# One joined first stage, its loads in order of need, and identity matmuls at the end of two attentions

## What is computed

```
x = x + L0_attn(layernorm(x))                 # softmax attention through 64 landmarks
x = x + L0_xattn(layernorm(x), ctx_512)       # 16 heads of 16: causal self-attention + attention to the context
x = x + L0_ffn(layernorm(x))                  # linear layer, x and weight rounded to a 6-bit grid in blocks of 32
x = x + L1_attn(layernorm(x))                 # attention on hyperbolic distances, masked by a threshold
x = x + L1_xattn(layernorm(x), ctx_512)       # 16 heads of 32, self and cross, each with an MLP
x = x + L1_ffn(layernorm(x))                  # 8 experts, the best 2 of each row
```

```
y = softmax(mask(q k^T / 4)) v                # first attention, 512 keys
y = y + softmax(qc kc^T / 4) vc               # second attention, 1024 keys of the context
return y @ Wp + bp
```

## Time and profile before

| | |
|---|---|
| median of 3 runs | 4172.58 us (4172.36 to 4176.27) |
| the profiled execution | 4168.0 us, span 4166.0 us |
| PE busy | 3411.4 us, 82% |
| DVE busy | 2071.5 us, 50% |
| ACT busy | 1641.3 us, 39% |
| POOL busy | 914.9 us, 22% |
| mean granted clock of PE | 0.914 |

### The profile page before, as it was taken

How to read it: one execution, slowest core, us unless ns; L and a number is a source line. 1 busy time by engine, 2 the same in 40 slices (tenths; PEclk the granted TensorE clock), 3 DMA queues, 4 the chain that set the end, 5 groups by cost and what they waited for, 6 DMA issues and landing times. The chain is left out here.

```text
span 4166.0 us, 56508 instructions
## 1 busy us (share of the span) xinstructions
PE 3411.4 (82%) x21678; PEld 1873.9 (45%) x21678; DVE 2071.5 (50%) x4222; ACT 1641.3 (39%) x2355; POOL 914.9 (22%) x955
## 2 busy tenths in 40 slices
PE   2888788898897688898887788988877888956997
PEld 2423554326325455245334535264235543345886
DVE  3464656553564654634556654634646556530111
ACT  1344654242343833333344742433437542411221
POOL 0210642001201822011104622012006420131111
PEclk9989899999998799999898899999997999967999
DMA  4121102201202012111112012011211121034444
GB/s 83 39 57 61 16 23 64 64 20 32 74 12 76 1 44 72 34 36 44 46 31 57 1 44 86 20 42 39 57 61 16 31 69 50 26 117 156 167 166 166
DMA packets 242482, 239.79 MB, mean 58 GB/s; under 512 B 111726, under 2 KB 209244, under 8 KB 239900
## 3 DMA queue, kind: packets, MB, share of 16 engines
q1 hardware_dynamic: 231344, 214.02, 17.7%
q10 hardware_dynamic: 7116, 11.77, 0.9%
q0 software_dynamic: 3744, 10.26, 0.6%
HBM read 167.24 MB, written 68.76 MB: 57 GB/s over the span
## 5 line engine op out<-in xcount | busy, mean ns | idle before, releaser
L864 ACT ACTIVATE prob<-psum 128x1024 f32<-128x1024 f32 x384 | 372.2, 1021 | 507.8 <-PE psum L782 507.8
L1202 ACT ACTIVATE prob<-psum 128x1024 f32<-128x1024 f32 (+3 forms) x384 | 331.5, 914 | 420.5 <-PE psum L1122 420.5
L910 DVE TENSOR_REDUCE scr<-psum 128x1 f32<-128x512 f32 x576 | 368.9, 685 | 194.2 <-PE psum L769 190.5
L1241 DVE TENSOR_REDUCE stats<-psum 128x1 f32<-128x512 f32 (+3 forms) x576 | 333.4, 619 | 158.4 <-PE psum L1110 153.8
L1122 PE MATMUL psum<-stack 32*128 32x512 f32 (+3 forms) x1536 | 210.7, 619 | 49.1 <-ACT prob L1202 41.2
L779 PE MATMUL psum<-stack 32*128 32x512 f32 x1536 | 226.6, 660 | 15.3 <-ACT prob L864 10.4
L400 PE MATMUL psum<-ident 128*128 128x128 f32 x1832 | 224.2, 280 | 14.6 <-PEq L1830 9.6
L400 PEld LDWEIGHTS psum<-ident 128*128 128x128 f32 x1832 | 216.5, 195 | 25.3 <-issue 24.4
L812 PE MATMUL psum<-prob,ones_f 128*32 128x512 f32 x1536 | 201.4, 592 | 0.0
L1137 PE MATMUL psum<-prob,vbig 128*32 128x512 f32 (+3 forms) x1536 | 191.9, 573 | 4.3 <-ACT prob L1202 4.3
L2741 PE MATMUL psum<-xgT,ew 128*128 128x256 f32 x736 | 167.8, 387 | 18.0 <-DVE xgT L2789 18.0
(11 more groups left out here) (469 smaller groups left out, 6488.2 us busy)
## 6 DMA issues: line engine op xcount, KB each, us to landing
ew<-in_L_ffn_W SPq DMA_DIRECT2D x46, 1024.0 KB, 7.5
stack<-q_terms SPq DMA_DIRECT2D x144, 128.0 KB, 2.6
w_mlp<-in_L_xattn_a_li_w SPq DMA_DIRECT2D x16, 1024.0 KB, 7.0
q_terms<-parts SPq DMA_DIRECT2D x96, 128.0 KB, 2.2
stack<-k_terms SPq DMA_DIRECT2D x72, 128.0 KB, 3.0
w_mlp<-k_terms SPq DMA_DIRECT2D x36, 256.0 KB, 4.5
w_mlp<-a_terms SPq DMA_DIRECT2D x36, 256.0 KB, 5.0
a_keys<-stack SPq DMA_DIRECT2D x4, 2048.0 KB, 6.3
```

The lines of the kernel that those rows point to most:

```text
L864: act.activation(prob[:, i % 4, :, :], psum[:, 2 * p:2 * p + 2, :], ACT.Exp, scale=scale).then_inc(exped, 1)
L910: dve.tensor_reduce(found[:, c:c + 1], ring(i), AX.X, ALU.max).then_inc(freed, 1)
L1202: act.activation(prob[:, i % 4, :, q0:T], psum[:, 2 * p:2 * p + 2, q0:T], ACT.Exp, scale=scale).then_inc(exped, 1)
L1241: dve.tensor_reduce(found[:, c:c + 1], ring(i)[:, 0:keys_of(t)], AX.X, ALU.max).then_inc(freed, 1)
```

## The change

**First piece.** The stages "clear", "load" and "qw" become one, "start" (from L266 of the new file on). Its engines do the following.

- SP issues 37 DMAs in this order: the matrix of the linear layer, `x`, the three weights of the first attention, the four weights of the attentions with heads of 16 as whole rows into a scratch tile (`unpadded`), and then 28 "late" ones. These count on the semaphore `loads`, and nobody waits for it in this stage.
- ACT issues the context, three biases and 21 small vectors (rows, no longer columns), and then copies the four weights from the scratch tile into their padded places, and the columns from PSUM.
- POOL clears the padded tiles and makes the masks; DVE fills, copies, and rounds the matrix as soon as that has landed; PE transposes the small vectors and the matrix.

The late loads are waited for by SP in "Asm", ahead of `load_kv`.

**Second piece.** At the end of `narrow_heads`, thus in "Ba" and "Bca", PE gets 3, 2 and 6 calls of `keep_running`.

```
+            sp.dma_start(xa[:, 0:KT, :], dram["L0_ffn_weight"]...).then_inc(linear_in, 16)
+            load_x(sp, slice(0, 1))
+            load_qkv(sp, 0)
+            for w, source, raw in heads:
+                sp.dma_start(raw[:, 0:w.shape[1], :], source).then_inc(raw_in, 16)
+            late(wBv[:, :, :], dram["L0_xattn_Wv"].rearrange("(k p) n -> p k n", p=P))
+            late(wBcv[:, :, :], dram["L0_xattn_Wcv"].rearrange("(k p) n -> p k n", p=P))
+            sp.wait_ge(zeroed, 2)
...
+            act.wait_ge(raw_in, 16 * len(heads))
+            act.wait_ge(zeroed, 6)
+            for w, _source, raw in heads:
+                k = w.shape[1]
+                act.copy(w[:, :, :].rearrange("p k (h w) -> p (k h) w", w=W)[:, :, D16:W],
+                         raw[:, 0:k, :].rearrange("p k (h d) -> p (k h) d", d=D16))
+            act.wait_ge(small_turned, 1)
...
+            pool.memset(wBp[:, :, :], 0.0).then_inc(zeroed, 1)
+            pool.memset(wDo[:, :, :], 0.0).then_inc(zeroed, 1)
+            pool.wait_ge(cleared, 4)
...
+            for w, _source, _raw in heads:
+                pool.memset(w[:, :, :], 0.0).then_inc(zeroed, 1)
...
+            dve.wait_ge(shaped, 5)
...
+            dve.wait_ge(linear_in, 16)
             quantise(dve, then, xa[:, 0:KT, :], KT, xo[:, 0:KT, :], xh[:, 0:KT, :],
...
@@ narrow_heads
+                keep_running(pe, 3, 3)
                 gather(HG - 1)
+                keep_running(pe, 2, 3)
                 spread_inverses(pe, HG - 1, inverted, spread_in)
+                keep_running(pe, 6, 3)
...
@@ landmark_attention
         @block.sync
         def _(sp):
+            sp.wait_ge(e.loads, 16 * e.n_late)
             e.load_kv(sp)
```

More of the change, by code:

```diff
@@ L224, in spread @@
         return v.partition_broadcast(P)
[L227 to L334, removed]
@@ L373, in _ @@
             then = chained(dve, dc)
-            then(dve.tensor_tensor(colB[:, 0, :], colB[:, 0, :], colB[:, 1, :], ALU.add))
+            dve.memset(columns_in, 0.0).then_inc(blanked, 1)
+            dve.memset(ident[:, :], 1.0).then_inc(cleared, 1)
+            dve.memset(avg[:, :], float(H) / 128.0).then_inc(cleared, 1)
+            dve.memset(prob[:, 2, 0, 0:P], FAR).then_inc(cleared, 1)
+            dve.memset(prob[:, 2, 1, 0:P], -BIG).then_inc(cleared, 1)
+            dve.memset(ones_f[:, :], 1.0)
+            dve.memset(minus_one[:, :], -1.0)
+            dve.memset(ones_b[:, :], 1.0)
+            dve.memset(nhalf[:, :], -0.5)
+            dve.wait_ge(shaped, 5)
+            strips = ident[:, :].rearrange("p (j w) -> p j w", w=W)
+            dve.tensor_copy(pads_of[:, :], strips[:, :, D16])
+            dve.tensor_copy(identb[:, :], ident[:, :])
+            dve.tensor_copy(hide_below[:, :], prob[:, 2, 0, 0:P])
+            dve.tensor_copy(hide_above[:, :], prob[:, 2, 1, 0:P])
+            dve.wait_ge(linear_in, 16)
             quantise(dve, then, xa[:, 0:KT, :], KT, xo[:, 0:KT, :], xh[:, 0:KT, :],
@@ L377, in _ @@
             dve.sem_inc(quant, 1)
+            dve.wait_ge(columns, 1)
+            for j in range(J):
+                dve.memset(colQK[W * j:W * j + 1, 1, :], 1.0)
+                dve.memset(colQK[W * j:W * j + 1, 3, :], 1.0)
+            dve.tensor_tensor(colB[:, 0, :], colB[:, 0, :], colB[:, 1, :], ALU.add)
         @block.tensor
         def _(pe):
-            pe.transpose(psum[:, KT, 0:n_cols], vectors, ident[0:n_cols, 0:n_cols])
-            pe.transpose(psum[:, KT + 1, 0:NE * FT], expert_biases, ident[0:NE * FT, 0:NE * FT])
+            pe.wait_ge(shaped, 1)
+            pe.wait_ge(small_in, 16 * n_small)
+            pe.transpose(psum[:, KT, 0:n_rows], columns_in, ident[0:n_rows, 0:n_rows])
+            pe.transpose(psum[:, KT + 1, 0:NE * FT], expert_biases, ident[0:NE * FT, 0:NE * FT]).then_inc(small_turned, 1)
             pe.wait_ge(quant, 1)
@@ L387, in _ @@
             last.then_inc(turned, 1)
-        @block.scalar
-        def _(act):
-            act.wait_ge(turned, 1)
-            act.copy(wC[:, :, :], psum[:, 0:KT, 0:C])
-            act.copy(cols[:, 0:n_cols], psum[:, KT, 0:n_cols])
-            act.copy(b1c[:, :, :].rearrange("p e f -> p (e f)"), psum[:, KT + 1, 0:NE * FT])
     def keep_running(pe, times, bank, at=3 * P):
@@ L1335, in decoder_layers @@
     e.keep = sb("keep", [P, P])
+    e.loads, e.n_late = loads, n_late[0]
     e.x_pair, e.c_all, e.vbig_all, e.prob_all, e.parts_all = x_pair, c_all, vbig_all, prob_all, parts_all
```

65 lines of the change are left out of this document (64 added, 1 removed).

## The result

The changed kernel takes 4125.15 us (median of 4 runs, 4113.20 to 4126.69), against 4172.47 us for the kernel before in the same job: a ratio of 0.9883 (95% interval 0.987 to 0.9896), 47 us or 1.1% faster. The forecast was 4102.5 us with a range of 4086 to 4122. The direction was right; the time lies 3 us above the range and 23 us above the forecast.

The account below looks back on a forecast made before the run. Bounds: a start chain slowed by small-piece loads, and PE at half clock at the ends of "Ba" and "Bca". 4168.0 - 44.3 - 25.8 = 4097.9 us, plus 4.6 us carried over: 4102.5 us, range 4086 to 4122.

Parts of the forecast that it names:

- The start, transfer path decides: First stage: queued transfers hold up SP's issues, PE begins the batch at 27.4 us, and the start gives 44.3 us.
- a choice between two bounds: First stage: 6.3 MB moved before SP is free, between SP issuing all ahead and only one load ahead.
- run ahead freely: Rival, first stage: SP's issues are not held up, PE begins at 19.7 us, time 4095 us; chance 0.20.
- the queue did not drain so slowly: Rival, first stage: at 183 GB/s PE begins at 37.7 us, time 4113 us; chance 0.16.
- SP's issues averaging more than 1 us: Sign in the first stage that would show the forecast to be wrong.
- The other engines under SP's cover: First stage: the other engines are done by about 19 us, ACT's weight copies by about 18 us, hidden under SP's issues.
- The rounding, which the prediction feared for: First stage: POOL's memsets beside DVE's rounding might stretch the computing path by up to 3.2 us, to 22.2 us.
- The clock at the eight places: Ends of "Ba" and "Bca", four batches: identity matmuls keep PE's clock full, giving 26.5 us less 0.7, 25.8 us.
- That it falls all the same: Rival, ends of "Ba" and "Bca": the clock falls in half or all places, 4123 to 4144 us; chance 0.13.
- what then waits elsewhere: After the joined start: ACT's four weight copies stay hidden, and SP's wait for late loads in "Asm" costs nothing.
- The carried-over 4.6 us: Whole kernel: the median lies 4.6 us above the profiled execution, added to 4097.9 us to give 4102.5 us.
- "Some us" for shifting half-clock stretches: Whole kernel: an earlier start shifts half-clock stretches against the work, sized by the batches' spread of 4.6 to 8.2 us.

Follow-up runs that it names:

- only_fill: The kernel before with only the three new `keep_running` lines added, its first three stages unjoined: 4148.98 us, ratio 0.9954.
- only_start: The changed kernel without the three new `keep_running` lines, so only the joined first stage: 4144.65 us, ratio 0.9942.
- repeat: The changed kernel unaltered, run again: 4122.84 us, ratio 0.9892 against the kernel before.
- start_pool_32: The joined first stage without the new `keep_running` lines, plus 32 tiny memsets on POOL ahead of the loop: 4128.97 us, ratio 0.9899.
- pool_32_timed: The changed kernel plus 32 tiny memsets on POOL ahead of the loop: 4108.61 us, ratio 0.9859.
- fill_turn: The changed kernel plus six loads moved to ACT, 32 POOL memsets, and identity matmuls at waits in "Asm", "Ba" and "Bca": 4062.87 us, ratio 0.9743.

## Why the prediction was wrong

**The start, transfer path decides: right, 3.1 us short.** PE begins at 30.5 us instead of 27.4 (30.8 to 32.4 us in the other kernels with this stage unchanged on SP). Named as the end were SP's issues, and they are. The bytes, 8.07 MB, were right, and so was the rate: between 2.5 and 26.6 us 6.15 MB moved, 255 GB/s, where 6.3 MB at 261 were taken. What was mis-sized is when SP is let go: its last issue ended at 29.3 us instead of 26.6, with 6.71 MB moved and not 6.3, and from there to PE it took 1.2 us, not 0.8. That 6.3 MB must have moved was a choice between two bounds, so that it came this close is in part luck. The four `wBp` loads took 2.97 us to issue, the last four rows 6.74. Neither rival on the queue came true: SP does not run ahead freely (4095 us), and the queue did not drain so slowly that PE began at 37.7 us (4113 us). A sign of being wrong was to be SP's issues averaging more than 1 us; they average 0.77 (28.5 us for 37).

**The other engines under SP's cover: right, 4 us later than said.** They ended at 22.75 us, not 19, since PE had to wait for the small vectors until 20.6 us, and DVE's casts waited for POOL:

```profile
3.95 3.14 DVE L364 COPY pads_of<-ident 128x4 f32<-128x4 f32 x1 [2.22 <-POOL prob L345]
4.03 3.12 DVE L365 CAST identb<-ident 128x128 bf16<-128x128 f32 x1
4.17 3.06 DVE L366 CAST hide_below<-prob 128x128 bf16<-128x128 f32 x1
...
7.14 0.21 DVE L367 CAST hide_above<-prob 128x128 bf16<-128x128 f32 x1
```

Three end together at 7.1 us, when POOL's padded memsets end; the one behind takes 0.21 us. The rule of the Trainium skill (SBUF — State Buffer, Who interferes with whom) on the ports that DVE and GpSimd share, which the prediction weighed, agrees with these rows in that the copies are held while POOL works; the rule speaks of one instruction, and here they are held through four memsets in a row (3.87 to 7.06 us). The rounding, which the prediction feared for, began at 7.27 us, behind them. As the stage's end was SP's, all this cost nothing. `load_kv` in "Asm" was not late.

**The clock at the eight places: right.** 25.8 us forecast, 26.2 measured, and 114.5 us for the eight places (114.6 at most) in all twelve profiles of kernels with these lines. That it falls all the same (4123 to 4144 us), the rival with 0.13, happened nowhere. That the sum came out within 0.4 us is in part luck, since the fourth batch's 5.5 us were an estimate. Whether the whole 26 us arrive in the time is open: by the medians the lines gave 18 us (`only_fill`, interval 12 to 27), 22 us (`only_start` to `repeat`) and 20 us (`start_pool_32` to `pool_32_timed`).

**The step that failed: that nothing else changes.** The sum, 4168.0 - 44.3 - 25.8, took the rest of the loop as it was, without a reason; "what then waits elsewhere" named ACT's copies and the late loads, not POOL's jump back. Joining the stages took 12 instructions from POOL's stream up to that jump, and it became some 2 us longer three times (2.3 to 3.4 us instead of 0.8 to 1.0), with PE waiting for the result and then longer at half clock. In the rows this costs 7 to 11 us up to L1905; in the time it cost 10 to 14 us, measured by making the jump short and changing nothing else. With 3.1 us for the start this brings the 4102.5 us to 4116 to 4120.

**The carried-over 4.6 us and the width.** The remaining 3 to 10 us are within what executions of one kernel differ by. The profiled execution of before was 4.6 us under its median and that of the change 12 us. "Some us" for shifting half-clock stretches was too little: single executions span 28 us in `repeat`. A range that took this in would have reached beyond 4125 us.

## What to carry to other kernels

A loop's jump back belongs to the stages on both sides of it: after any change ahead of a loop or in it, compare for each engine the time from its branch to its next instruction, because here the number of POOL's instructions alone moved POOL's. Where PE falls to half clock behind a wait, look at the work behind it and not only at the wait (here a 3.8 us wait was followed by some 20 us at half speed), and try the longest wait ahead of dense work first: here the filler paid though it ran partly at half clock itself. And where the clock makes executions of one kernel differ by 28 us, a sum of terms from one profile needs that width, and pieces should be timed each by itself.

## What was not expected of the hardware

- POOL's jump back took from 0.23 to 3.39 us, by where it stands in POOL's stream; 12 instructions made 2 us of it. In the same traces DVE's took 0.58 to 0.61 us, ACT's 0.41 to 0.51 and PE's 0.42 to 0.52, moved or not.
- A queue that holds SP back leaves ACT's free: the same six loads that took SP 8.9 us were issued by ACT in 3.4 us.
- The identity matmuls held the clock at the ends of the attentions in every batch of twelve profiles, though 12 calls at a longer wait (`fill_turn`) did not keep it from falling there, but had it back before the transposes.
